# Products without a use in three of TensorE's waits while the gates are computed

## The chip, the cores and the metric

The kernel runs on one core of a Trainium2 chip. A core has four compute engines with instruction streams of their own: TensorE (PE, matrix products and transposes, results in the banks of PSUM), VectorE (DVE), ScalarE (ACT) and GpSimd (POOL); SyncE (SP) starts the transfers. Engines wait for each other by semaphores. The metric is the device time of one execution in microseconds, the median of several runs.

## The reference

The input x is 32 sequences of 128 tokens with 128 features, and ctx has the same shape. Four steps are added to x, each scaled by the tanh of a gate; cut to what matters:

```
x = x + tanh(g_xattn[0]) * mlstm(layernorm(x), ctx, ctx, ifgate_w, ifgate_b, outnorm_w)
x = x + tanh(g_ffn[0])   * quantized_ffn(layernorm(x), W1, b1, W2, b2)
x = x + tanh(g_xattn[1]) * dtw_align(ctx, layernorm(x))
x = x + tanh(g_ffn[1])   * gated_experts(layernorm(x), gate_weight, w1, b1, w2, b2)
```

The change lies in the first step. Its part that matters:

```
pre   = 15 * tanh((concat(q, k, v) @ ifgate_w.T + ifgate_b) / 15)
i_pre, f_pre = pre[..., :8], pre[..., 8:]
lf_cs = cumsum(log_sigmoid(f_pre))
log_d = lf_cs[t] - lf_cs[s] + i_pre[s]        for s <= t, else -inf
m     = max over s of log_d
d_mat = exp(log_d - m);  scores = q @ k.T / 4;  s_mat = scores * d_mat
h     = s_mat @ v / (max(|sum of s_mat|, exp(-m)) + 5e-5)
```

## The kernel before, in words

The order of the work is written out by hand, one stream for each engine; nothing is planned by a scheduler. The 32 sequences are called blocks b, and four of them a group g.

In the prelude TensorE turns ctx and the normed x (turn_ctx L1364, turn_x L1372), sums the gates' inputs (L1380, L1388) and turns these sums (turn_sums, L1395). Then comes what is called the chain of the gates here, in which each step waits for the one before:

- VectorE adds the bias (L870), ScalarE takes the tanh (L479), exponential (L481) and logarithm (L482) and signals nlf_ready. TensorE meanwhile makes spread(0), two small products (L1346, L1348) for the scales of the quantized weights.
- TensorE multiplies by a triangle of ones, the cumulative sum over tokens (L1417, into bank 5).
- VectorE forms a = input gate plus cumulative sum and repeats it (L880, L881, L886), and signals a_ready.
- TensorE turns a: eight transposes, four for each half (L1421, into banks 0 and 1).
- VectorE copies the halves (L890) and scans for the running maximum (L893, eight scans, m_ready counts them).
- TensorE turns the maxima: four transposes after four scans, four after eight (L1426, banks 2 and 3).
- VectorE splits a and m into three bf16 parts (left_over, L900, with ScalarE's L495 and L497 in between), subtracts the turned maxima (L910, which reads L1426's banks), and makes mblk (L735, called from L917), which signals mblk_ready.

Behind L1426 the kernel already has `keep_warm(7, 16)`: 16 products of 128 x 128 weights with 512 columns in bf16 into bank 7, whose result nobody reads (L1342). It stands behind a wait for scale_ready, which VectorE gives early. Then TensorE waits for m_tok_ready, mblk_ready, part_ready and others, and starts the attention. For each block b it makes exponents (L1445, L1447, L1450), scores (L1459), and for earlier blocks weigh (L1469) and turn (L1478); ScalarE takes the exponential (L510), and VectorE multiplies (L928). In each engine's stream an instruction that waits holds up all that stand behind it. Bank 4, which the change writes, was last read by ScalarE's copy of the first gate sums (L460) and is next written by the scores.

Of the kernel before, what the change touches and what calls it, by code (L numbers as in the profile page):

```python
# [55 lines left out]
def program(nc, x, ctx_, g_x, g_f, if_w, if_b, on_w, a_w1, a_b1, a_w2, a_b2, gate_w, m_w1, m_b1, m_w2, m_b2, out):  # L56
    with ExitStack() as stack:
# [176 lines left out]
        def bank(n, a=0, b=512):  # L234
            return PS[:, n, a:b]
# [12 lines left out]
        def rep(ap, n):  # L248
            return ap.unsqueeze(1).to_broadcast([ap.shape[0], n, ap.shape[1]])
# [1087 lines left out]
        def _(pe):  # L1337


            def keep_warm(n, products):  # L1340
                for _ in range(products):
                    pe.matmul(bank(n), identb[:], rep(neg[:], 4), start=True, stop=True)  # L1342

            def spread(n):
                pe.wait_ge(S["mm_ready"], n + 1)
                pe.transpose(PS[0:2, 7, 0:P], mm[:, 0:2], identf[:]).then_inc(S["mm_turned"], 1)  # L1346
                pe.wait_ge(S["mm_global"], n + 1)
                pe.matmul(bank(7, P, P + 2), ones[0:2, :], gq[0:2, 2:4], start=True, stop=True).then_inc(S["mm_spread"], 1)  # L1348
# [43 lines left out]
            def turn_sums(n):  # L1392
                pe.wait_ge(S["gates_kept"], n + 1)
                for k in range(4):
                    ins = pe.transpose(bank(2 + n, P * k, P * k + P), sums[:, n, P * k:P * k + P], identf[:])  # L1395
                ins.then_inc(S["gates_turned"], 1)
# [16 lines left out]
            query_sums(1)  # L1413
            turn_sums(1)
            spread(0)
            pe.wait_ge(S["nlf_ready"], 1)
            pe.matmul(bank(5, 0, B * NH), tri[:], nlf.rearrange("p b h -> p (b h)"), start=True, stop=True).then_inc(S["cumsum_done"], 1)  # L1417
            pe.wait_ge(S["a_ready"], 1)
            for j in range(2):
                for g in range(4):  # L1420
                    ins = pe.transpose(bank(j, P * g, P * g + P), A[:, 12288 + P * (4 * j + g):12288 + P * (4 * j + g + 1)], identf[:])  # L1421
                ins.then_inc(S["a_turned"], 1)
            for j in range(2):
                pe.wait_ge(S["m_ready"], 4 * (j + 1))
                for g in range(4):
                    ins = pe.transpose(bank(2 + j, P * g, P * g + P), av[:, 1, 4 * j + g, :], identf[:])  # L1426
                ins.then_inc(S["m_turned"], 1)
# [314 lines left out]
```

## Time and profile before

| what | us |
|---|---|
| median of 3 runs | 744.48 (743.02 to 745.78) |
| the profiled execution's own time | 743.02 |
| its span | 741.1 |
| PE busy | 569.4 (77%) |
| DVE busy | 569.1 (77%) |
| ACT busy | 408.5 (55%) |
| POOL busy | 128.3 (17%) |

The span is from the first to the last instruction that the profiler sees. Busy shares are averages over stages that differ: the attention (62 to 150 us) and the experts (from about 395 us) are the stages in which PE works nearly without a break. The granted clock is TensorE's alone: 1.00 is the level of 2.4 GHz, 0.50 that of 1.2 GHz. "Issue" in the chain is time for which the profile has no releaser. A row's start and duration are in us; several instructions of one line that follow each other are merged into one row.

### The profile page before, as it was taken

How to read it: one execution, taken by the hardware profiler on the slowest of the kernel's cores; microseconds unless marked ns; L12 is line 12 of the kernel's file. 1: busy time of each engine (PE TensorE's matmuls, PEld its weight loads, DVE VectorE, ACT ScalarE, POOL GpSimd, SP SyncE). 2: the span in 40 equal slices, each digit the busy share in tenths (PEclk: the TensorE clock that was granted, in tenths of full speed). 3: DMA queues.
4: the chain of work that ended last, by engine and by line, in shares of the span. 5: the costliest groups of instructions: out<-in, count | busy, mean ns of one | idle time of the engine just before them, and what ended most of it. 6: DMA issues, size and time to landing. Idle time of an engine off the chain costs nothing.

```text
span 741.1 us, 17115 instructions
## 1 busy us (share of the span) xinstructions
PE 569.4 (77%) x6351; PEld 402.0 (54%) x6419; DVE 569.1 (77%) x1737; ACT 408.5 (55%) x766; POOL 128.3 (17%) x163
## 2 busy tenths in 40 slices
PE   2758998826544720083679999999999999999997
PEld 2433444312244620073576777777777777777776
DVE  6867788998969559997974566586877888887775
ACT  2667876678862532265445565665545454545452
POOL 3000343413000000000036777700000000000000
PEclk9959999957858975578758999999999999999999
DMA  8100000000010000041000000000000000010000
GB/s 227 42 0 1 3 3 2 2 0 0 1 56 2 2 2 0 0 119 54 0 1 1 2 1 2 2 1 2 16 1 3 14 0 15 0 42 0 15 1 16
DMA packets 19676, 12.13 MB, mean 16 GB/s; under 512 B 1149, under 2 KB 18457, under 8 KB 19609
## 3 DMA queue, kind: packets, MB, share of 16 engines
q1 hardware_dynamic: 19608, 11.25, 5.5%
q8 instruction: 40, 0.66, 0.4%
q14 instruction: 28, 0.22, 0.1%
HBM read 9.15 MB, written 2.10 MB: 15 GB/s over the span
## 4 chain that ended last, share of the span: by engine, by line
PE 63%; DVE 25%; ACT 6%; issue 3%; SPq 1%; DMA 1%; another core or an unknown queue 0%; DVEq 0%
PE PS L1649 9%; PE PS L1664 8%; PE PS L1666 8%; PE PS L1665 8%; PE PS L1650 7%; PE PS L1648 6%; DVE A L1175 3%; DVE Bm L1146 3%; PE PS L1459 3%; PE PS L1469 2%; DVE Bm L735 2%; PE PS L1577 1%; PE PS L1478 1%; DVE A L1140 1%; ACT A L455 1%
## 5 line engine op out<-in xcount | busy, mean ns | idle before, releaser
L698 ACT ACTIVATE A<-PS,small_t 128x512 f32<-128x512 f32 x256 | 168.1, 688 | 119.0 <-PE PS L1650 117.5
L1666 PE MATMUL PS<-kT_w,A 128*128 128x128 bf16 x1024 | 174.8, 219 | 0.0
L1665 PE MATMUL PS<-kT_w,A 128*128 128x128 bf16 x1024 | 174.8, 219 | 0.0
L1664 PE MATMUL PS<-kT_w,A 128*128 128x128 bf16 x1024 | 174.7, 219 | 0.0
L1277 DVE TENSOR_TENSOR A<-A 128x512 bf16<-128x512 f32 x192 | 123.6, 690 | 7.8 <-ACT A L698 6.6
L1664 PEld LDWEIGHTS PS<-kT_w,A 128*128 128x128 bf16 x1024 | 100.2, 98 | 7.4
L1665 PEld LDWEIGHTS PS<-kT_w,A 128*128 128x128 bf16 x1024 | 100.2, 98 | 7.4
L1666 PEld LDWEIGHTS PS<-kT_w,A 128*128 128x128 bf16 x1024 | 100.2, 98 | 0.0
L1649 PE MATMUL PS<-A,xn_w 128*128 128x512 bf16 (+1 forms) x256 | 97.5, 381 | 3.5 <-issue 0.2
L1650 PE MATMUL PS<-A,xn_w 128*128 128x512 bf16 (+1 forms) x256 | 97.5, 381 | 0.0
L1285 DVE SCALAR_TENSOR_TENSOR xs<-PS,A,xs 128x128 f32 (+1 forms) x192 | 54.1, 343 | 49.2 <-PE PS L1666 49.1
L1648 PE MATMUL PS<-A,xn_w 128*128 128x512 bf16 (+1 forms) x193 | 73.5, 381 | 0.0
L413 POOL TENSOR_TENSOR A<-A 128x512 bf16<-128x512 f32 x64 | 64.5, 1040 | 22.4 <-ACT A L698 22.4
L1650 PEld LDWEIGHTS PS<-A,xn_w 128*128 128x128 bf16 x256 | 25.1, 98 | 30.7 <-issue 0.8
L1585 PE MATMUL PS<-identf,Bm 64*64 64x64 f32 x2 | 0.6, 298 | 51.6 <-DVE Bm L1146 51.6
L1648 PEld LDWEIGHTS PS<-A,xn_w 128*128 128x128 bf16 x256 | 26.7, 104 | 21.1 <-issue 0.6
L1649 PEld LDWEIGHTS PS<-A,xn_w 128*128 128x128 bf16 x256 | 25.1, 98 | 21.1 <-issue 0.6
L409 POOL TENSOR_TENSOR A<-A 128x512 bf16<-128x512 f32 x8 | 9.4, 1183 | 153.3 <-ACT A L691 153.3
L1585 PEld LDWEIGHTS PS<-identf,Bm 64*64 64x64 f32 x2 | 0.2, 125 | 51.9 <-issue 49.1
L1459 PE MATMUL PS<-A,kT_w 32*128 32x256 f32 x256 | 25.4, 435 | 3.7 <-DVE A L928 3.7
L702 ACT ACTIVATE Bm<-PS 128x512 f32 x16 | 9.6, 597 | 33.3 <-PE PS L1666 33.3
L928 DVE TENSOR_TENSOR A<-Bm,PS 128x512 f32<-128x512 f32 x32 | 20.6, 684 | 7.7 <-ACT Bm L510 4.8
(337 smaller groups left out, 1141.5 us busy)
## 6 DMA issues: line engine op xcount, KB each, us to landing
slab<-in_L_ffn_w_dram SPq DMA_DIRECT2D x16, 256.0 KB, 3.0
xs<-in_x_dram SPq DMA_DIRECT2D x4, 512.0 KB, 5.7
cs<-in_ctx_dram SPq DMA_DIRECT2D x4, 512.0 KB, 6.5
out_dram<-xs SPq DMA_DIRECT2D x8, 256.0 KB, 2.5
Bm<-in_L_ffn_W_dram SPq DMA_DIRECT2D x2, 256.0 KB, 2.9
b2blk<-in_L_ffn_b_dram SPq DMA_DIRECT2D x12, 4.0 KB
onw_b<-n_L_xattn_outnorm_w_dram SPq DMA_DIRECT2D x1, 64.0 KB
ab_b<-in_L_ffn_b_dram SPq DMA_DIRECT2D x1, 64.0 KB
```

The lines of the kernel that those rows point to most:

```text
L413: pool.tensor_tensor(hl[:, e % 2, c, :], hf[:, e % 2, c, :], hh[:, e % 2, c, :], ALU.subtract).then_inc(S["h_low_pool"], 1)
L698: act.activation(hf[:, e % 2, c, :], bank(c), ACT.Gelu_apprx_tanh, bias=b1).then_inc(S["h_gelu"], 1)
L1146: dve.tensor_tensor_scan(rt[:, s + 1, 1:RTW], mins[:, s], dd[:, s], rt[:, s + 1, 0:1], ALU.min, ALU.add).then_inc(S["row_done"], 1)
L1277: dve.tensor_tensor(hl[:, e % 2, c, :], hf[:, e % 2, c, :], hh[:, e % 2, c, :], ALU.subtract).then_inc(S["h_low_dve"], 1)
L1285: ins = dve.scalar_tensor_tensor(out=row, in0=bank(4 + e % 2, P * k, P * k + P), scalar=gate, in1=row, op0=ALU.mult, op1=ALU.add)
L1459: ins = pe.matmul(PS[:, 2 + r, 0:256], kT[rows, P * b:P * b + P], qTm[rows, :, P * b:P * b + P], start=True, stop=True)
L1648: pe.matmul(bank(c), w1h[:, e, c, :], x4h[:, xw], start=True, stop=False)
L1649: pe.matmul(bank(c), w1h[:, e, c, :], x4l[:, xw], start=False, stop=False)
L1650: pe.matmul(bank(c), w1l[:, e, c, :], x4h[:, xw], start=False, stop=True).then_inc(S["h_ready"], 1)
L1664: pe.matmul(o, hh[:, e % 2, c, t], w2h[:, e, c, :], start=(c == 0 and k == 0), stop=False, skip_group_check=True)
L1665: pe.matmul(o, hh[:, e % 2, c, t], w2l[:, e, c, :], start=False, stop=False, skip_group_check=True)
L1666: ins = pe.matmul(o, hl[:, e % 2, c, t], w2h[:, e, c, :], start=False, stop=(c == NC - 1), skip_group_check=True)
```

## The change

TensorE's stream gets three more calls of keep_warm, all into bank 4: six products ahead of the wait for nlf_ready, six ahead of the wait for a_ready, and eight ahead of the first wait for m_ready. Nothing else is changed, on any engine.

```
             query_sums(1)
             turn_sums(1)
             spread(0)
+            keep_warm(4, 6)
             pe.wait_ge(S["nlf_ready"], 1)
             pe.matmul(bank(5, 0, B * NH), tri[:], nlf.rearrange("p b h -> p (b h)"), start=True, stop=True).then_inc(S["cumsum_done"], 1)
+            keep_warm(4, 6)
             pe.wait_ge(S["a_ready"], 1)
             for j in range(2):
                 for g in range(4):
                     ins = pe.transpose(bank(j, P * g, P * g + P), A[:, 12288 + P * (4 * j + g):12288 + P * (4 * j + g + 1)], identf[:])
                 ins.then_inc(S["a_turned"], 1)
+            keep_warm(4, 8)
             for j in range(2):
                 pe.wait_ge(S["m_ready"], 4 * (j + 1))
```

TensorE's stream before, from spread(0) to the start of the attention (slab holds the logarithms, tri the triangle of ones, A both a and the maxima, neg and identb are constants):

```order
 L1346 MATMUL PS<-identf,mm 2x128
 L1348 MATMUL PS<-gq,ones 128x2
 L1417 MATMUL PS<-slab,tri 128x256
 L1421 MATMUL PS<-identf,A 128x128 x8
 L1426 MATMUL PS<-identf,A 128x128 x8
 L1342 MATMUL PS<-neg,identb 128x512 x16
 L1445 MATMUL PS<-Bm,slab 64x512 x4
```

The cumulative sum and both sets of transposes stand next to each other, and all products without a use stand behind them.

The same place of the stream now; three lines are added above, so L1417 is now L1418, L1421 is L1423, L1426 is L1429, and L1445 is L1448:

```order
 L1346 MATMUL PS<-identf,mm 2x128
 L1348 MATMUL PS<-gq,ones 128x2
 L1342 MATMUL PS<-neg,identb 128x512 x6
 L1418 MATMUL PS<-slab,tri 128x256
 L1342 MATMUL PS<-neg,identb 128x512 x6
 L1423 MATMUL PS<-identf,A 128x128 x8
 L1342 MATMUL PS<-neg,identb 128x512 x8
 L1429 MATMUL PS<-identf,A 128x128 x8
 L1342 MATMUL PS<-neg,identb 128x512 x16
 L1448 MATMUL PS<-Bm,slab 64x512 x4
```

Six products now stand ahead of the cumulative sum, six between it and the first transposes, and eight ahead of the second ones; each group has to be through before the instruction behind it can run.

## Rows read from the trace of the kernel before

**Rows 1.** The page: the span.
```profile
span 741.1 us, 17115 instructions
```

**Rows 2.** The chain that ended last, 38 to 66 us: start, duration, what.
```profile
54.94 5.07 PE PS L1342 x16
60.01 1.77 issue
61.78 0.41 PE PS L1445 x4
```

**Rows 3.** VectorE in order of time, 39 to 70 us: start, duration, instruction, idle before.
```profile
50.41 0.69 DVE L890 COPY A<-PS 128x512 f32<-128x512 f32 x1 [0.16 <-PE PS L1421]
51.13 2.63 DVE L893 TENSOR_TENSOR_SCAN A<-A 128x128 f32<-128x128 f32 x8
...
56.18 0.61 DVE L910 TENSOR_TENSOR expnm<-slab,PS 128x64 f32<-128x64 f32 x4
...
60.00 1.67 DVE L735 TENSOR_SCALAR Bm<-A,hneg 128x1024 bf16<-128x1024 bf16 x4
```

**Rows 4.** TensorE in order of time, 0 to 60 us: the four steps.
```profile
42.64 0.58 PE L1348 MATMUL PS<-gq,ones 2*128 2x2 f32 x2 [0.74 <-DVE gq L735]
45.13 1.22 PE L1417 MATMUL PS<-slab,tri 128*128 128x256 f32 x2 [1.91 <-ACT slab L482]
48.40 1.97 PE L1421 MATMUL PS<-identf,A 128*128 128x128 f32 x8 [2.05 <-DVE A L886]
52.56 2.38 PE L1426 MATMUL PS<-identf,A 128*128 128x128 f32 x8 [2.19 <-DVE A L893]
```

**Rows 5.** L1342: form, parts of its 16 products, then windows with the granted clock.
```profile
L1342 PE MATMUL PS<-neg,identb x16: 379/474/634, 54.7 to 59.6; 128*128 128x512 bf16 x16
...
54.73 2.77 PE L1342 MATMUL PS<-neg,identb 128*128 128x512 bf16 x6
...
58.12 1.89 PE L1342 MATMUL PS<-neg,identb 128*128 128x512 bf16 x8
...
38.00:57.90 19.90, 12.16 (x45) 0.50 0.00 0
58.30:59.80 1.50, 1.50 (x8) 1.00 0.00 0
```

**Rows 6.** TensorE in order of time: the same four transposes at clock 1.00 and 0.50.
```profile
32.82 0.60 PE L1395 MATMUL PS<-identf,Bm 128*128 128x128 f32 x4
...
40.57 1.12 PE L1395 MATMUL PS<-identf,Bm 128*128 128x128 f32 x4 [0.70 <-ACT Bm L460]
```

**Rows 7.** TensorE behind two idle times; stretches with the granted clock (third from last).
```profile
175.08 1.46 PE L1516 MATMUL PS<-Bm,slab 128*128 128x512 bf16 x3 [3.25 <-ACT Bm L589]
...
174.20:176.00 1.80, 0.92 (x3) 0.38 (x4) 1.80 (x2) 1.10 (x3) 0.00 (x0) 0.50 0.00 0
...
189.36 0.81 PE L1516 MATMUL PS<-Bm,slab 128*128 128x512 bf16 x3 [2.44 <-ACT Bm L589]
...
188.00:191.00 3.00, 1.64 (x8) 0.92 (x10) 2.96 (x2) 2.52 (x6) 0.00 (x0) 1.00 0.00 0
```

**Rows 8.** TensorE in the attention, a block at clock 1.00 and one at 0.50.
```profile
71.35 0.41 PE L1445 MATMUL PS<-Bm,slab 64*64 64x512 bf16 x4
72.12 0.71 PE L1459 MATMUL PS<-A,kT_w 32*128 32x256 f32 x8
...
73.70 0.41 PE L1445 MATMUL PS<-Bm,slab 64*64 64x512 bf16 x4
...
126.49 0.64 PE L1445 MATMUL PS<-Bm,slab 64*64 64x512 bf16 x4
127.92 1.23 PE L1459 MATMUL PS<-A,kT_w 32*128 32x256 f32 x8
...
130.32 0.41 PE L1445 MATMUL PS<-Bm,slab 64*64 64x512 bf16 x4
...
126.40:129.70 3.30, 3.30 (x34) 1.38 (x36) 1.87 (x6) 2.61 (x7) 0.00 (x0) 0.50 0.00 0
```

More of the change, by code:

```diff
@@ L1415, in _ @@
             spread(0)
+            keep_warm(4, 6)
             pe.wait_ge(S["nlf_ready"], 1)
             pe.matmul(bank(5, 0, B * NH), tri[:], nlf.rearrange("p b h -> p (b h)"), start=True, stop=True).then_inc(S["cumsum_done"], 1)
+            keep_warm(4, 6)
             pe.wait_ge(S["a_ready"], 1)
@@ L1422, in _ @@
                 ins.then_inc(S["a_turned"], 1)
+            keep_warm(4, 8)
             for j in range(2):
```

## The prediction

> **What bounds the kernel now.** I read the busy shares first, then the chain that ended last, then TensorE's and VectorE's rows in order of time around the edit, then the granted clock. The span is 741.1 us [rows 1]; the program's own time in that execution is 743.02 us, so 1.9 us lie around the span, and the median of the three runs, 744.48, is 1.46 above it. I add my sum to both. Only some 20 us of the span can be touched directly, 43 to 66 us: the chain of the gates and the start of the attention.
>
> In the chain the work goes to and fro [rows 2, 4]: ScalarE ends the logarithm, TensorE makes the cumulative sum, VectorE spreads it, TensorE turns it (L1421), VectorE copies and scans (L890, L893), TensorE turns the maxima (L1426) and makes its 16 products without a use (L1342). The last step that really releases the attention isn't TensorE: the chain shows 1.77 us of "issue" from 60.01 to 61.78, and VectorE's rows [rows 3] say what it was. From 51.13 VectorE has no idle time: scan, left_over (L900), the subtraction that reads the turned maxima (L910, starts at 56.18), and four products for mblk (L735, from 60.00 for 1.67 us, so to 61.67). TensorE waits for mblk_ready and starts L1445 at 61.78. From the scan on, TensorE is off the path: L1426 is done at 54.94 [rows 2], L910 reads it only at 56.18, 1.24 us of slack.
>
> TensorE's three waits [rows 4] are 1.91 us (before L1417), 2.05 us (before L1421) and 2.19 us (before L1426). From 38 to 57.9 us the granted clock is 0.50, the level of 1.2 GHz; it is back at 1.00, 2.4 GHz, while the 16 products run [rows 5]. So the edit's aim is seen: raise the clock earlier.
>
> **The change part by part.** *Price of a product.* In the slow level six start within 2.77 us; the longest row is 0.634 us, so five intervals are 2.77 - 0.634 = 2.14, 0.427 us each. In the fast level eight end in 1.89 us; less one of 0.379 that is seven intervals, 0.216 each [rows 5].
>
> *First six, before L1417.* They run in the slow level, since TensorE has had little work for several us: 6 x 0.427 = 2.56 us. They can start when L1348 leaves the array, between 43.0 and 43.22 [rows 4], and end at 45.57 to 45.78; L1417 started at 45.13, with 0.17 us of weight load ahead of it that can hide under the last product. Delay: 0.65 at most, 0.3 at least. I take 0.45 us, all on the path.
>
> *L1417 itself* stays in the slow level (1.22 us): no gain. If the clock were already up, at most half of it, 0.6; I keep that in the low end only.
>
> *Second six, before L1421.* In the slow level throughout 2.56 us, starting some 0.2 under the end of L1417, against a wait of 2.05: 0.3 us late. With the clock up in their midst they fit. TensorE now has unbroken work from 43.0 on, and before the change the clock rose in the midst of the 16 products, behind eight slow ones. So the rise comes here most likely. I take 0, bounds 0 and 0.3.
>
> *L1421, eight transposes, on the path.* Four transposes of the same kind cost 0.60 us at clock 1.00 and 1.12 at 0.50 (L1395, both in the trace) [rows 6]; eight then go from 1.97 to about 1.05. But the second L890 copy also waits for the first copy, which takes 0.69 after the first four: 0.60 + 0.05 + 0.69 = 1.34 instead of 2.01 from L1421's start (48.40 to 50.41). Gain 0.67; bounds 0 (clock still low) and 0.92. I take 0.65.
>
> The Trainium skill, "TensorE: Matmul & The Clock Gate", section "Part 4: PE-mode transpose", says that the full clock does not engage for transposes. The pair of L1395 disagrees on their speed, 1.12 against 0.60 us. By the rule the 0.65 would be nothing and the sum would be 0.65 us higher.
>
> *Third, eight products before L1426.* Fast: 1.73 us in a wait of 2.19. Slow: 3.4 us, about 1.0 late, which the slack of 1.24 before L910 covers. I take 0. L1426 in the fast level saves 0.5 us off the path: nothing.
>
> *The 16 products that were there.* This is where I expect the price. Before, half of them ran in the slow level and they lasted to 60.01, so TensorE idled only 1.77 us before the attention and entered it at clock 1.00. Now they all run in the fast level. VectorE's chain is 0.65 - 0.45 = 0.2 us earlier, so the last maxima come near 53.6 instead of 53.8, their four transposes take 0.6, and 16 x 0.216 = 3.45 us of products end near 57.6. VectorE still needs until 61.5. The idle time before L1445 grows from 1.77 to about 3.9 us. What the clock does in such gaps can be read elsewhere in this trace [rows 7]: after an idle time of 2.44 us (before L1516 at 189.36) the clock was still 1.00; after 3.25 us (before L1516 at 175.08) it was at 0.50. At 3.9 us I expect it to fall, before the attention or just as it starts.
>
> *Price of the fall.* One block of the attention lasts 2.35 us at clock 1.00 (L1445 at 71.35 and at 73.70) and 3.83 us where the clock was 0.50 nearly throughout (126.49 and 130.32), 1.48 more [rows 8]. At the start TensorE also waits for ScalarE's exponentials, which hides part: the least is the longer exponents of the first block, L1445 to L1459, 0.77 us warm (71.35 to 72.12) and 1.43 cold (126.49 to 127.92), 0.66 more. The most is two blocks in the slow level, 3.0. I take one block, 1.5 us, which is nearest to what the row at 126.49 shows: the clock rose again after one block's work.
>
> *Sum:* +0.45 + 0 - 0.65 + 0 + 1.5 = +1.3 us. On the profiled execution 744.3; on the median 744.48 + 1.3 = 745.8 us, 0.17% more. About 0.5%, 3.7 us, is what a measurement of this kernel can tell from no change, so I forecast no measurable change, leaning slower.
>
> **The rivals.**
> A, *the clock holds across the longer gap.* For it: 2.44 us of idle did not drop it, and products may end later than I think. Against: 3.25 us did drop it, and this gap is longer. Then only -0.2 us stays, at best 0.3 - 0.92 - 0.6 = -1.2: 744.3 us, down to 743.3.
>
> B, *the clock isn't up in time for L1421* (or transposes gain nothing, the rule above). For it: six slow products and L1417 may not suffice. Then +0.45 + 0.3 in the chain, the 16 products end later since part of them or of the eight before them is slow, the gap is shorter, and the fall costs nothing: 745.2 us. Against: TensorE's work is unbroken for over 5 us.
>
> C, *slower, one mechanism: the fall before the attention and a start in the slow level that does not end after a block.* At L1445 TensorE still waits between exponents and scores for ScalarE and VectorE, so its work has holes, and a clock that has fallen may stay down, as it does from 38 to 57.9 us with work and holes [rows 5]. From the third slow block on it passes 3.7 us: 3 x 1.48 - 0.2 = +4.2, 748.7 us; four blocks 750.2. Against: at 126.49 the clock rose after one block, and slow work leaves fewer holes.
>
> D, *faster by over 0.5%.* No term here reaches 3.7 us. It would need later falls of the clock (as at 126 us, 1.48 us a block) to vanish because all that follows is shifted by some tenths; three would have to go at once.
>
> **How the numbers follow.** Forecast 0.55, with its own range from the bounds: 0.3 - 0.92 + 0.66 = 0 to 0.65 + 0.3 + 3.0 = +3.95, so 744.5 to 748.4. A 0.22, B 0.09, C 0.09, D 0.05. The low end takes in A and the scatter of the three runs (743.02 to 745.78, 1.4 either way): 742.2. The high end takes the forecast's upper bound and C's first step: 748.9. Faster by over 0.5%: D and the scatter, 0.07. Slower by over 0.5%: C and the forecast's upper edge, 0.13. Within: 0.80.
>
> **What would show it.** L1417's start, measured from the end of the logarithm on ScalarE, should grow by about 0.45 us; if not, the first six were cheaper than 0.427 each. Clock 1.00 before the transposes of L1421, and these eight in about 1.05 us, show the gain; the second L890 copy should start 1.3 us behind them. VectorE should stay unbroken from the scan to mblk. The idle time before the attention should be near 3.9 us instead of 1.77, with the clock at 0.50 behind it and the first one or two blocks at up to 3.8 us. A clock of 1.00 through the start of the attention would refute the forecast and leave A; more than two slow blocks would be C. A difference above 0.5% either way with all of this in place would mean that the time moved somewhere that I haven't looked.

## The result, and the profile after

| | us |
|---|---|
| changed kernel, median of 22 runs | 745.6 (744.16 to 750.35) |
| kernel before, median of 22 runs | 743.37 (740.45 to 745.78) |
| ratio | 1.0041, 95% interval 1.003 to 1.0052 |
| span of the profiled execution, after | 743.3 (before 741.1) |

The changed kernel is slower by 0.41%, some 3.05 us; the interval of the ratio is 2.2 to 3.9 us, and the two medians lie 2.2 us apart. The forecast was 745.8 us, +1.3 us, no measurable change leaning slower, range 742.2 to 748.9. The time lies in the range and the difference below 0.5%; but the difference is about twice what I had summed (1.7 times by the medians, 2.3 times by the ratio), so terms of the sum were wrong or missing.

TensorE of the changed kernel in order of time (start, duration, instruction, idle before), to be held against [rows 2, 4, 5]:

```profile
42.48 0.58 PE L1348 MATMUL PS<-gq,ones 2*128 2x2 f32 x2 [0.74 <-DVE gq L735]
42.99 2.74 PE L1342 MATMUL PS<-neg,identb 128*128 128x512 bf16 x6
45.53 1.06 PE L1418 MATMUL PS<-slab,tri 128*128 128x256 f32 x2
46.38 2.28 PE L1342 MATMUL PS<-neg,identb 128*128 128x512 bf16 x6
48.64 1.10 PE L1423 MATMUL PS<-identf,A 128*128 128x128 f32 x8
49.57 1.89 PE L1342 MATMUL PS<-neg,identb 128*128 128x512 bf16 x8
...
53.84 3.62 PE L1342 MATMUL PS<-neg,identb 128*128 128x512 bf16 x16
61.30 0.41 PE L1448 MATMUL PS<-Bm,slab 64*64 64x512 bf16 x4 [3.85 <-DVE Bm L735]
63.64 0.64 PE L1448 MATMUL PS<-Bm,slab 64*64 64x512 bf16 x4
67.03 0.41 PE L1448 MATMUL PS<-Bm,slab 64*64 64x512 bf16 x4
69.38 0.41 PE L1448 MATMUL PS<-Bm,slab 64*64 64x512 bf16 x4
```

The waits before the sum and before the first transposes are gone. The eight transposes take 1.10 us instead of 1.97. The 16 products take 3.62 us, and in place of the "issue" of 1.77 us the attention now waits 3.85 us, released by VectorE's mblk. Each L1448 row of four products begins a block.

Its granted clock (stretch, TensorE busy, clock third from last):

```profile
43.00:47.80 4.80, 4.80 (x13) 0.50 0.01 2
48.10:49.60 1.50, 1.50 (x12) 1.00 0.00 0
...
54.00:57.50 3.50, 3.46 (x17) 1.00 0.00 0
57.60:61.00 3.40, 0.00 (x0) 1.00 0.00 0
61.20:65.00 3.80, 3.70 (x32) 0.56 0.02 4
65.20:69.00 3.80, 3.72 (x60) 1.00 0.00 0
```

The clock rises before the transposes, 10 us earlier than before the change, holds through the products and the idle time, and falls as the attention begins. In another execution of the same kernel (after_again, below) it fell earlier and stayed down longer:

```profile
57.60:61.00 3.40, 1.27 (x12) 0.72 0.00 0
61.20:65.00 3.80, 3.80 (x29) 0.50 0.02 6
65.20:69.00 3.80, 3.80 (x40) 0.50 0.00 0
```

VectorE of the changed kernel answers to [rows 3]:

```profile
49.34 1.29 DVE L890 COPY A<-PS 128x512 f32<-128x512 f32 x2 [0.75 <-PE PS L1423]
50.66 2.63 DVE L893 TENSOR_TENSOR_SCAN A<-A 128x128 f32<-128x128 f32 x8
```

It has no idle time from the scan on, as before; from the transposes' start to the scan it is 2.02 us instead of 2.73.

### The profile page after: what moved, and what is told of

It is laid out like the page before. It is cut to its first block, busy times and chain, and to the rows that moved or that the text cites. A ratio compares the mean times of both kernels' runs of the same rounds, so it can differ in the third digit from the quotient of the medians.

```text
span 743.3 us, 17223 instructions
## 1 busy us (share of the span) xinstructions
PE 584.3 (79%) x6439; PEld 407.3 (55%) x6439; DVE 569.4 (77%) x1737; ACT 408.7 (55%) x766; POOL 128.4 (17%) x163
## 4 chain that ended last, share of the span: by engine, by line
PE 64%; DVE 26%; ACT 6%; issue 2%; SPq 1%; DMA 1%; DVEq 0%
PE PS L1667 8%; PE PS L1669 8%; PE PS L1668 8%; PE PS L1651 7%; PE PS L1652 7%; PE PS L1653 7%; DVE A L1175 3%; DVE Bm L1146 3%; PE PS L1462 3%; PE PS L1472 2%; DVE Bm L735 2%; PE PS L1580 1%; PE PS L1481 1%; DVE A L1140 1%; ACT A L455 1%
## 5 line engine op out<-in xcount | busy, mean ns | idle before, releaser
L698 ACT ACTIVATE A<-PS,small_t 128x512 f32<-128x512 f32 x256 | 168.4, 687 | 119.7 <-PE PS L1653 118.2
L1652 PE MATMUL PS<-A,xn_w 128*128 128x512 bf16 (+1 forms) x256 | 98.0, 383 | 0.0
L1653 PE MATMUL PS<-A,xn_w 128*128 128x512 bf16 (+1 forms) x256 | 97.9, 383 | 0.0
L1651 PE MATMUL PS<-A,xn_w 128*128 128x512 bf16 (+1 forms) x256 | 97.9, 382 | 0.0
L702 ACT ACTIVATE Bm<-PS 128x512 f32 x16 | 9.6, 597 | 33.3 <-PE PS L1669 33.3
L928 DVE TENSOR_TENSOR A<-Bm,PS 128x512 f32<-128x512 f32 x32 | 20.6, 684 | 8.6 <-ACT Bm L510 4.8
```

Of the source, the lines that this page charges most:

```text
L698: act.activation(hf[:, e % 2, c, :], bank(c), ACT.Gelu_apprx_tanh, bias=b1).then_inc(S["h_gelu"], 1)
L1651: pe.matmul(bank(c), w1h[:, e, c, :], x4h[:, xw], start=True, stop=False)
L1652: pe.matmul(bank(c), w1h[:, e, c, :], x4l[:, xw], start=False, stop=False)
L1653: pe.matmul(bank(c), w1l[:, e, c, :], x4h[:, xw], start=False, stop=True).then_inc(S["h_ready"], 1)
```

## The experiments

All are variants of the four numbers of products: ahead of the sum, of the transposes of a, of those of the maxima, and of the attention. Before is 0/0/0/16, the change 6/6/8/16. Each code fence is cut to the lines that differ: bridge against the changed kernel, no_first_bridge and fit_bridge against bridge, fit_align against fit_bridge, and short_last, third_only and first_only against the kernel before. For each profile I also give how far the fourth block of the attention starts behind the first (before: 61.78 to 69.00, 7.22 us; the changed kernel: 8.08).

**bridge, 6/6/8/32.** Does the longer idle time cost?

```
             pe.wait_ge(S["scale_ready"], 1)
-            keep_warm(7, 16)
+            keep_warm(7, 32)
```

> The changed kernel, with 32 instead of 16 products ahead of the attention; 16 x 0.216 = 3.46 us more of products, from 57.5 to about 60.9, which still end before mblk is ready at 61.2. Theory G (the idle time of 3.85 us lets the clock fall and the attention starts slow): the clock stays at 1.00 from 48 us through the attention's start, its first L1448 still starts at about 61.3, the third one at about 66.3 instead of 67.03, and the time is 0.7 to 1.5 us below the changed kernel, 743.4 to 744.5 on the scale of before at 743.4. Rival H (the added products cost in the chain itself, or by something later, and the gap does not matter): the clock may change but the time stays with the changed kernel, ratio to before near 1.003 to 1.004.

Measured: 743.32 us, ratio 0.9996 (0.998 to 1.0012). TensorE in order of time, the first and the fourth block:

```profile
53.35 7.07 PE L1342 MATMUL PS<-neg,identb 128*128 128x512 bf16 x32
60.81 0.41 PE L1448 MATMUL PS<-Bm,slab 64*64 64x512 bf16 x4 [0.39 <-issue]
...
68.04 0.41 PE L1448 MATMUL PS<-Bm,slab 64*64 64x512 bf16 x4
```

And its stretches with TensorE's busy time and the granted clock:

```profile
48.00:60.70 12.70, 11.04 (x56) 1.00 0.00 0
60.90:66.00 5.10, 4.37 (x64) 1.00 0.02 5
```

The clock stays up and the fourth block is 7.23 us behind the first. The interval lies below that of the changed kernel. Sixteen more products with no use take its loss away, so the loss isn't the products' own time.

**bridge_again and after_again**, both on one chip in one session.

> The kernel with 32 products ahead of the attention once more, beside the changed kernel on one chip. Theory G: the clock stays at 1.00 from the transposes of the gates through the attention's start, fourth block 7.2 us behind the first, ratio 0.998 to 1.001, 1.5 to 3.5 us below the changed kernel. Rival I: not more than 1 us below it.

> The changed kernel unchanged, on the same chip and with the same runs of before as the next one. Theory G: the idle time before the attention is 3.8 to 3.9 us, the clock is at 0.50 somewhere between 58 and 66 us, and the start of the fourth block lies 8.1 us (one slow stretch caught late) to 10.6 us (all three blocks slow) behind that of the first, against 7.2 with a fast clock; ratio 1.002 to 1.005. Rival I (the clock's fall costs only the 0.86 us of the profile of the changed kernel, and the rest of the ratio 1.0041 is chance): ratio 1.000 to 1.002.

Measured: bridge 744.04 us, ratio 1.0009 (0.999 to 1.0029); the changed kernel 746.75 us, ratio 1.0058 (1.0037 to 1.008). The intervals are apart again; 0.49%, 3.6 us, lie between the two ratios, and 2.7 us between the two medians. The profile of after_again is the one with the long slow stretch above; its blocks:

```profile
59.73 0.64 PE L1448 MATMUL PS<-Bm,slab 64*64 64x512 bf16 x4 [3.84 <-DVE Bm L735]
62.39 0.64 PE L1448 MATMUL PS<-Bm,slab 64*64 64x512 bf16 x4
66.72 0.64 PE L1448 MATMUL PS<-Bm,slab 64*64 64x512 bf16 x4
70.24 0.41 PE L1448 MATMUL PS<-Bm,slab 64*64 64x512 bf16 x4
```

10.51 us from the first to the fourth, 3.29 more than with a fast clock: rival I falls, and the one profile of the changed kernel with its 0.86 us had caught a mild case. Of one kernel, the same idle time costs 0.9 or 3.3 us. In these two profiles it goes with the moment at which the clock falls: inside the idle time here (0.72 from 57.6 to 61.0 us), as the first block starts in the other.

**after_third**, a third profile of the changed kernel.

> The changed kernel, one more look at the clock at the attention's start. Theory G: 3.8 to 3.9 us of idle time before it, clock at 0.50 at some time between 58 and 70 us, fourth block between 8.0 and 10.6 us behind the first. Rival A of the prediction (the clock sometimes holds over this gap): 7.2 us.

Idle time 3.85 us, clock 0.58 from 61.2 to 65.0 us, first block at 60.75 and fourth at 68.95: 8.20 us. In all three profiles the clock fell; rival A was never seen.

**short_last, 0/0/0/8.** The idle time alone, nothing in the gates.

```
-            keep_warm(7, 16)
+            keep_warm(7, 8)
```

> The kernel before with 8 instead of 16 products ahead of the attention, nothing added. They end near 58.2, and the idle time before the attention is 3.6 us, with no other change. Theory G: the clock is at 0.50 in the attention's first 3 us or more, the third block's L1445 starts 0.7 to 1.5 us later than 66.66, ratio 1.001 to 1.003. Rival H: the gap does not matter, ratio 1.000.

Measured: 744.25 us, ratio 1.002 (1.0004 to 1.0035). TensorE at the first and the fourth block:

```profile
60.29 0.64 PE L1445 MATMUL PS<-Bm,slab 64*64 64x512 bf16 x4 [3.92 <-DVE Bm L735]
...
70.60 0.41 PE L1445 MATMUL PS<-Bm,slab 64*64 64x512 bf16 x4
```

Idle time 3.92 us, and 10.31 us for three blocks. Removing eight unused products from the kernel before costs 3.1 us there, with nothing changed ahead of it. That isolates the idle time as a cause. In the whole time less of it is seen: the medians are 0.5 us apart, the ratio says 0.2%, and its interval is only just above 1.

**third_only, 0/0/8/16.**

```
+            keep_warm(4, 8)
             for j in range(2):
                 pe.wait_ge(S["m_ready"], 4 * (j + 1))
```

> Only the eight products ahead of L1426 are added; 16 stay ahead of the attention. Theory G: no delay in the chain of the gates (the maxima are turned up to 1 us later, within their slack), no gain at L1421 (clock 0.50), the products end near 57.5 to 59 instead of 60.0, idle time 2.5 to 4 us before the attention; where it is over 3 us the clock falls and the attention's first blocks cost 0.7 to 1.5 us: ratio 1.001 to 1.002. Rival H: with no product in the chain the time is that of before, ratio 1.000.

Measured: 745.74 us, ratio 1.002 (1.0005 to 1.0036). In its profile the eight products ran slow (3.62 us), the maxima were turned 1 us later without moving VectorE, the idle time was 3.27 us, and the blocks took 10.57 us. The ratio is what theory G said, though this fall cost 3.35 us and not 0.7 to 1.5; its median is 2.0 us above that of before.

**first_only, 6/0/0/16**, one profile.

```
+            keep_warm(4, 6)
             pe.wait_ge(S["nlf_ready"], 1)
```

> The kernel before with only the six products ahead of the cumulative sum. Theory: in the slow level L1418 starts 0.3 to 0.5 us after the logarithm has ended instead of 0.05, and what follows up to the attention is later by this; products alone do not raise the clock lastingly, so the eight transposes of a take about 1.97 us. Rival: six products and the sum are enough, and the transposes take 1.1 us.

TensorE in order of time:

```profile
42.66 2.21 PE L1342 MATMUL PS<-neg,identb 128*128 128x512 bf16 x6
44.95 1.22 PE L1418 MATMUL PS<-slab,tri 128*128 128x256 f32 x2
48.23 1.97 PE L1422 MATMUL PS<-identf,A 128*128 128x128 f32 x8 [2.05 <-DVE A L886]
...
54.55 4.78 PE L1342 MATMUL PS<-neg,identb 128*128 128x512 bf16 x16
61.60 0.41 PE L1446 MATMUL PS<-Bm,slab 64*64 64x512 bf16 x4 [2.27 <-DVE Bm L735]
63.61 0.58 PE L1446 MATMUL PS<-Bm,slab 64*64 64x512 bf16 x4 [0.52 <-ACT Bm L510]
```

The stretch behind it, with the granted clock:

```profile
63.80:67.00 3.20, 3.20 (x32) 0.50 0.03 8
```

Here the clock was still up when the six began, so they took 2.21 us and did not delay the sum at all; the transposes were slow again, as expected. And the clock fell in the attention behind an idle time of only 2.27 us and one of 0.52, 8.06 us for three blocks. So the limit that I had read between 2.44 and 3.25 us [rows 7] is no limit.

**no_first_bridge, 0/6/8/32.**

```
-            keep_warm(4, 6)
             pe.wait_ge(S["nlf_ready"], 1)
```

> Without the six products ahead of the cumulative sum; six, eight and 32 stay. Theory: no delay of the sum (0.05 us after the logarithm); TensorE's unbroken work then begins 2.1 us later, so the clock is at 1.00 for the eight transposes of a in some executions and not in others (1.1 or 2.0 us); the attention starts 0.2 us later to 0.7 us earlier than before, in the fast level; ratio 0.999 to 1.0005. Rival (the first six are what raises the clock in time): the transposes take 2.0 us, and the six products before them are 0.3 us late.

Measured: 743.46 us, ratio 1.0008 (0.999 to 1.0025). The transposes ran in 1.06 us: in this execution the first six weren't needed. The attention starts 0.7 us earlier in relation to ScalarE's tanh than in the kernel before.

**fit_bridge, 4/6/8/32, and fit_bridge_again.**

```
-            keep_warm(4, 6)
+            keep_warm(4, 4)
             pe.wait_ge(S["nlf_ready"], 1)
```

> As with 32 products ahead of the attention, and four instead of six ahead of the cumulative sum: 4 x 0.427 = 1.71 us fit in the wait of 1.91 us. Theory G: L1417's successor starts when the logarithm ends, 0.4 us earlier, the transposes still run in the fast level (1.1 us for eight), and the attention starts 0.5 to 0.9 us earlier than in the kernel before and in the fast level: ratio to before 0.9985 to 0.9995. Rival H: ratio 1.002 to 1.004 still.

> The 4/6/8/32 version once more, for its time. Theory G: attention starts 18.4 to 18.9 us after the tanh of the gates' sums begins on ScalarE, against 19.6 before, with a fast clock; fourth block 7.2 us behind the first; ratio 0.998 to 1.000. Rival J (what the chain gains is given back by clock falls further on): ratio 1.000 to 1.001.

Measured: 743.74 us, ratio 0.9997 (0.9981 to 1.0014), and 743.4 us, 0.9998 (0.9985 to 1.0012). Locally all is as expected: the attention starts 18.4 us behind the tanh instead of 19.6, in the fast level, blocks 7.22 us. Yet nothing is left of 1.2 us in the time, as rival J says. A first place where it goes is the attention itself, where TensorE stops for VectorE's L928 near 120 us. Before:

```profile
120.74 0.41 PE L1445 MATMUL PS<-Bm,slab 64*64 64x512 bf16 x4
124.30 1.30 PE L1459 MATMUL PS<-A,kT_w 32*128 32x256 f32 x8 [2.71 <-DVE A L928]
```

and fit_bridge:

```profile
119.35 0.41 PE L1448 MATMUL PS<-Bm,slab 64*64 64x512 bf16 x4
122.94 1.82 PE L1462 MATMUL PS<-A,kT_w 32*128 32x256 f32 x8 [2.75 <-DVE A L928]
...
130.09 0.41 PE L1448 MATMUL PS<-Bm,slab 64*64 64x512 bf16 x4
```

From the block ahead of this stop to the second one behind it, it is 9.58 us before (120.74 to 130.32) and 10.74 here. Before, the clock falls at 126.4 us, behind the stop, and is at 0.50 for 3.4 us; here it falls at 122.2 us, inside the stop, and is at 0.50 for 6.9 us. The same stretch takes 9.6 us in before_look, in bridge and in all three profiles of the changed kernel, and 10.5 to 10.7 us in bridge_again, no_first_bridge, fit_bridge_again and fit_align. It isn't the early start alone that does it: first_only, whose attention starts as before, has 10.9. Where it is long, an attention that started up to 1.2 us earlier has given nearly all of it back at 155 us: ScalarE's L443 starts 112.5 us behind the tanh in both profiles of 4/6/8/32, and 112.6 before.

**before_look**, the kernel before again.

> The kernel before, one more look. Theory G: its 16 products end between 59.3 and 61 us depending on when the clock rises among them; idle time 0.8 to 2.3 us; fourth block 7.2 us behind the first where the clock holds, 8.1 where the gap is near 2.3 us.

Idle time 2.05 us, clock held, blocks at 61.71 and 68.93. A second place lies far behind the attention, in the turns of the distances (L1577). There 256 small f32 products stand in the code, each of which is two in the trace, so 512. Before_look:

```profile
251.57 2.73 PE L1577 MATMUL PS<-A,Bm 64*32 64x68 f32 x132 [1.27 <-issue]
254.99 2.58 PE L1577 MATMUL PS<-A,Bm 64*32 64x68 f32 x128 [0.69 <-issue]
258.72 2.60 PE L1577 MATMUL PS<-A,Bm 64*32 64x68 f32 x128 [1.15 <-issue]
262.18 2.50 PE L1577 MATMUL PS<-A,Bm 64*32 64x68 f32 x124 [0.86 <-issue]
```

The changed kernel, whose L1580 is the same line:

```profile
252.58 2.34 PE L1580 MATMUL PS<-A,Bm 64*32 64x68 f32 x112 [1.27 <-issue]
256.14 2.62 PE L1580 MATMUL PS<-A,Bm 64*32 64x68 f32 x128 [1.21 <-issue]
259.59 2.61 PE L1580 MATMUL PS<-A,Bm 64*32 64x68 f32 x128 [0.83 <-issue]
263.05 2.62 PE L1580 MATMUL PS<-A,Bm 64*32 64x68 f32 x128 [0.84 <-issue]
266.77 0.53 PE L1580 MATMUL PS<-A,Bm 64*32 64x68 f32 x16 [1.11 <-issue]
```

TensorE stops for 0.6 to 1.6 us after each 128 products (all profiles), and the profile names nothing that it waits for. The code has a wait here, for ScalarE's copies (dist_kept), from the fifth group of 56 on; in the kernel before that is behind 224, 280, 336 products and so on, while the pauses stand behind 132, 260 and 388, and ScalarE's L637 itself waits for TensorE in them. The first stretch is 132 less the number of added products: 132 with none, 140 with eight fewer, 126 with six, 124 with eight, 112 with 20, 102 with 30, 98 with 34, 96 with 36. With five or more, by this count, and with six or more in the profiles, a fifth stretch and a fourth inner pause appear. In the changed kernel's transfers from 251 to 268 us only instructions move:

```profile
q8 instruction: 4, 0.07, 1.6%
```

Four pieces of some 17 KB in 17 us, one for each 128 products; it is four in the kernel before too. There they begin to move at 253.3, 257.6, 261.6 and 265.1 us, and TensorE goes on 2.4 to 2.7 us behind each of the first three (256.02, 260.02, 264.03). By the Trainium skill, "Advanced Engine Details and Errata", section "ISA Cache", a line of that cache holds 16 KB or 256 instructions, and there are two. 128 products with their weight loads are 256 instructions, so the trace agrees in number and size of a line; the same section gives 32 KB for an engine but 128 KB for TensorE, and how many lines there are no run here shows. That the pauses are waits for instructions is my reading of the count, the transfers and the shift with every added product; the profile names no releaser.

**fit_align, 4/6/8 and 128 short products.** If the place of the pauses counts, still more instructions should be faster: with 130 added the first boundary comes after two products, where no pause is expected, since none is seen after four products in the kernel before, whose first stretch is 4 + 128.

```
-            keep_warm(7, 32)
+            for _ in range(128):
+                pe.matmul(bank(7, 0, 112), identb[:], neg[:, 0:112], start=True, stop=True)
```

> The 4/6/8/32 version, with the last 32 products of 512 columns replaced by 128 products of 112 columns, about as long in all (some 7 us in the fast level). TensorE's stream before the turns of the distances (L1577) is then longer by 130 products than in the kernel before, instead of 34. Theory F (TensorE pauses once in 128 products of the turns, at places fixed by their number from the program's start; 5 to 128 added products bring a fifth stretch, 129 to 132 do not): the stretches of the turns are 130, 128, 128 and 126 products, four instead of five, they last 12.6 to 13.9 us instead of 14.5 to 15.0, and the time is about 1.2 us below that of the 4/6/8/32 version, ratio to before 0.997 to 0.999. Rival K (every added product costs something on the way, wherever it stands): five stretches or longer ones, ratio 1.000 or above.

TensorE in order of time, the short products and the turns:

```profile
51.97 6.46 PE L1434 MATMUL PS<-neg,identb 128*128 128x112 bf16 x128
...
250.42 2.69 PE L1581 MATMUL PS<-A,Bm 64*32 64x68 f32 x130 [1.26 <-issue]
254.08 2.57 PE L1581 MATMUL PS<-A,Bm 64*32 64x68 f32 x128 [0.98 <-issue]
258.08 2.55 PE L1581 MATMUL PS<-A,Bm 64*32 64x68 f32 x128 [1.44 <-issue]
261.81 2.57 PE L1581 MATMUL PS<-A,Bm 64*32 64x68 f32 x126 [1.18 <-issue]
```

Four stretches of 130, 128, 128 and 126, 13.96 us from the first start to the end, as theory F said, instead of five in 14.81 and 15.00 us with 4/6/8/32; by the stretches rival K falls. The time was 741.8 us against 742.68 of before, ratio 0.9985 (0.9969 to 1.0001), span 739.0. It is the best version measured, but two things are not shown: that it beats the kernel before, since the interval touches 1, and that it beats 4/6/8/32 by what the pauses cost, since the intervals of the three overlap. In its profile the attention starts 1.2 us earlier than before, 0.9 of it is given back behind the stop at 120 us, and the turns are no shorter than in the kernel before (14.18 and 13.11).

## Why the prediction came out as it did

The changed kernel was profiled three times, the kernel before twice. Means of the parts in us, beside the forecast; where three values stand, they are those of after, after_third and after_again:

| term | forecast | measured |
|---|---|---|
| first six products | +0.45 | +0.56 in one profile, 0 in two |
| the cumulative sum itself | 0 | -0.17, -0.53, 0; mean -0.2 |
| second six | 0 | 0 |
| transposes of a | -0.65 | -0.71 |
| third eight | 0 | 0 |
| fall of the clock before the attention | +1.5 | +0.86, +0.98, +3.29; mean +1.71 |
| turns of the distances | not seen | +1.26 |
| start of the attention, behind ScalarE's tanh: the first five rows together | -0.2 | -0.3, -1.2, -0.7; mean -0.7 |

*What was right.* The mechanism that carried the forecast: the idle time before the attention grew to 3.85 us (3.9 said), the clock fell in it or at its end in every profile, and taking the idle time away (bridge) or making it alone (short_last) moved the time as it should. VectorE bounds from the scan on, and L1426's slack swallowed what the third group did. The gain at L1421 was priced well, 0.71 for 0.65; the transposes follow the clock, 1.10 against 1.97 us, against the rule of the Trainium skill, "TensorE: Matmul & The Clock Gate", section "Part 4: PE-mode transpose", as far as their speed goes. Whether transposes help to keep the clock up no run here shows.

*First six products.* The step "they run in the slow level" was right in one execution of three. In the other two the clock was at 1.00 when they began, and the sum started 0.06 us after the logarithm, as before. I had taken the state of the one profile for that of the kernel; 0 was outside my bounds of 0.3 to 0.65. In one of them the sum itself then ran in the fast level and saved 0.53 us (L1418 in 0.70 instead of 1.22), which I had kept for the low end only.

*Price of the fall.* One block's 1.48 us was near the mean, but not a typical case: it was either about 0.9 or over 3. Two variants with a similar idle time, short_last (3.92 us) and third_only (3.27), had 3.1 and 3.35. Such cases may be the long tail of the changed kernel's times, 747 to 750 us; no profile shows one of those. My upper bound of 3.0 was a little short, and C, three slow blocks, is what after_again shows, though it cost 3.3 us and not 4.4: the three blocks took 0.65, 1.46 and 1.18 us longer than in the kernel before. In the first of them, a wait of 0.53 us for ScalarE's L510 that stands in the kernel before is gone, and the third ended in the fast level.

*The range.* Its ends don't quite follow from their terms: A's lowest, 743.3, less the scatter of 1.4 is 741.9 and not 742.2, and the highest of the upper bound and C's first step is 748.7, not 748.9. Nothing hangs on it.

*What the sum left out.* The step "only some 20 us of the span can be touched directly, 43 to 66 us" was wrong. The 20 products that the change adds, with their weight loads 40 instructions, stand ahead of the turns and move the pauses there: from the first start of the turns to their end it is 14.18 and 13.11 us before, 14.72, 14.72 and 15.27 after, +1.26 in the mean. Two profiles of one kernel differ by over 1 us here, so the mean alone is weak; but all four profiles with four stretches have 12.75 to 14.18 us, and all ten with five have 14.64 to 15.29.

The sum of these means is -0.7 + 1.7 + 1.3 = +2.2 us (before rounding), as much as lies between the medians, of 3.05 by the ratio. ScalarE's rows say where the rest is. From its tanh to its first L702 in the experts (403.7 us in the kernel before) the three profiles of the changed kernel take 3.2 us longer in the mean than the two of before: +0.95 up to L546, at 76 us, which is the late start and the fall of the clock; +0.1 from there to the turns; +1.26 in them; +0.4 from there to the first L698, at 396 us; and +0.5 from there to L702. The last is a step: 8.7 us in all three and in one of the two of before, 7.7 us in the other, where the clock rises at 396.0 us (in the changed kernel's profile it is 0.50 from 396.2 to 398.8 us). So it isn't the change's alone. Why these last 0.9 us are lost stays open.

Why the variants with a bridge tie with before, though their attention starts 0.7 to 1.2 us earlier, has then two parts: in four of five profiles the fall near 122 us takes 1.1 us of it, and the fifth stretch of the turns takes about as much. A profiled execution is only one of those in the median, and in these profiles the losses even exceed the gain, so the account is one of places and not of the last tenth.

## What to carry to other kernels

Products without a use keep the clock only if they reach up to the work that needs it; if a raised clock makes those that stand there shorter, their number has to grow with it, or the idle time just moves to a worse place. Count added instructions as a shift of everything behind them on that engine, and look in the profile for stretches whose idle time is put down to "issue" at even distances: whoever adds or removes instructions ahead of them moves the pauses. A gain at one place can be lost at the next fall of the clock, so follow another engine's rows from stage to stage before believing it. One profile of a kernel with clock changes shows one of several courses; take two or three before pricing one.

## What the runs showed of the hardware that I had not expected

In the turns TensorE pauses 0.6 to 1.6 us after each 128 products with weight loads where these follow each other every 20 ns (128 in 2.6 us), while 128 products of 112 columns in 6.46 us run without such a pause. The clock may be up or down at the same point of the same program: at the first six products of the changed kernel it was 0.50 in one execution and 1.00 at their start in two. And the clock fell behind an idle time of 2.27 us in one execution, when it held over one of 2.44 us elsewhere. The same stop of 2.7 us in the attention was followed by 3.4 us of slow clock in some profiles and by 6.9 us in others.
